# Selective scan in a four-layer kernel: read-out in half steps over seven groups, a fourth decay buffer, input loads in three pieces, and one group's decay products made twice

## The reference

```
delta = softplus(dt_proj(...))           # per token and channel d (256)
def step(h, inp):                        # h: 256 channels x 64 states
    dA = exp(dt[:, :, None] * A)
    h = dA * h + dt[:, :, None] * b[:, None, :] * xt[:, :, None]
    y = einsum('bdn,bn->bd', h, c)
```

## Time and profile before

| | us |
|---|---|
| median of 3 runs | 1350.41 (1347.94 to 1356.02) |
| the profiled execution: its own time | 1350.97 |
| its span, first to last instruction | 1349.1 |
| prepare stage, up to the first scan | 100.8 |
| scan stage, first scan to last | 622 |
| experts, attention, feed-forward | from about 758 to the end |

### The profile page before, as it was taken

One profiled execution on the slowest core, in us unless ns is written; L12 is line 12 of the kernel. 1 busy time (PEld: TensorE's weight loads), 2 busy tenths in 40 slices (PEclk: granted clock), 3 DMA queues, 4 the chain that ended last, 5 costly groups with the idle time before them and its releaser, 6 DMA issues.

```text
span 1349.1 us, 29055 instructions
## 1 busy us (share of the span) xinstructions
PE 1126.4 (83%) x11730; PEld 726.6 (54%) x11730; DVE 846.0 (63%) x1006; ACT 500.5 (37%) x1245; POOL 306.3 (23%) x930
## 2 busy tenths in 40 slices
PE   3647787889878887788886499999999597999998
PEld 2535444444444554454543288887777344465665
DVE  5859989899999999899995211112111477842211
ACT  3865554556555655555553011111111110121110
POOL 9641222222223222422232211111111200000000
PEclk8865868776888779876877599999999797999999
DMA  3897235433223222312214652222210400000000
GB/s 105 244 281 209 61 87 134 107 98 103 52 58 90 47 51 56 90 36 48 59 50 155 203 200 79 77 93 94 97 43 16 133 1 0 0 8 8 17 16 16
DMA packets 171685, 111.99 MB, mean 83 GB/s; under 512 B 93637, under 2 KB 162248, under 8 KB 169248
## 3 DMA queue, kind: packets, MB, share of 16 engines
q1 hardware_dynamic: 163120, 88.69, 23.7%
q0 software_dynamic: 8000, 20.87, 4.7%
q10 hardware_dynamic: 432, 0.59, 0.2%
HBM read 63.18 MB, written 45.90 MB: 81 GB/s over the span
## 4 chain that ended last, share of the span: by engine, by line
PE 52%; DVE 21%; issue 9%; SPq 7%; ACT 5%; DMA 3%; POOL 2%; DVEq 0%; POOLq 0%; ACTq 0%
DVE h L1151 13%; PE psum L1401 10%; PE psum L1413 10%; PE psum L1885 8%; PE psum L935 5%; PE psum L1896 4%; PE psum L921 4%; ACT decay L1036 3%; PE psum L902 3%; DVE den L1715 2%; PE psum L1841 2%; SPq L278 2%; DMA xdiag<-x_parts_d 1%; SPq L201 1%; SPq L199 1%
## 5 line engine op out<-in xcount | busy, mean ns | idle before, releaser
L1151 DVE TENSOR_TENSOR_SCAN h<-decay,psum 128x1024 f32<-128x1024 f32 x256 | 568.6, 2269 | 41.9 <-ACT psum L1046 34.5
L1036 ACT ACTIVATE decay<-psum 128x512 f32<-128x512 f32 x512 | 279.2, 600 | 211.1 <-PE psum L902 108.8
L921 PE MATMUL psum<-xdiag,bstat 96*128 96x64 bf16 x4096 | 199.9, 211 | 59.3 <-DVE h L1151 57.9
L921 PEld LDWEIGHTS psum<-xdiag,bstat 96*128 96x128 bf16 x4096 | 166.0, 109 | 86.7 <-DVE h L1151 77.3
L902 PEld LDWEIGHTS psum<-rows,shared 32*128 32x128 bf16 x4096 | 90.0, 104 | 221.2 <-issue 114.2
L935 PE MATMUL psum<-h,cstat 128*32 128x512 f32 x1024 | 187.2, 814 | 1.0 <-ACT y_raw L1088 1.0
L902 PE MATMUL psum<-rows,shared 32*128 32x64 bf16 x4096 | 123.9, 207 | 46.5 <-ACT decay L1036 38.0
L1401 PE MATMUL psum<-xdt,shared 128*128 128x320 f32 x512 | 141.4, 438 | 0.7 <-ACT xdt L1460 0.7
L1306 POOL TENSOR_TENSOR carry<-decay,h 128x16 f32<-128x16 f32 x240 | 57.9, 241 | 366.6 <-ACT decay L1036 366.4
L1413 PE MATMUL psum<-shared,hid 128*128 128x256 f32 x640 | 139.5, 379 | 0.6 <-ACT hid L1454 0.6
L1413 PEld LDWEIGHTS psum<-shared,hid 128*128 128x128 f32 x640 | 121.2, 190 | 17.0 <-issue 1.1
(11 more groups left out here) (192 smaller groups left out, 1044.1 us busy)
## 6 DMA issues: line engine op xcount, KB each, us to landing
shared<-in_w SPq DMA_DIRECT2D x16, 1024.0 KB, 4.8
xdiag<-x_parts_d SPq DMA_DIRECT2D x256, 48.0 KB
x_parts_d<-x_parts POOLq DMA_DIRECT2D x46, 256.0 KB, 8.0
parts_d<-dt_parts SPq DMA_DIRECT2D x24, 256.0 KB, 9.4
rows<-parts_d SPq DMA_DIRECT2D x128, 48.0 KB
disp_d<-zero SPq DMA_DIRECT2D x4, 1305.0 KB, 8.2
xd<-disp_d SPq DMA_DIRECT2D x8, 652.5 KB, 6.2
picked_d<-zero SPq DMA_DIRECT2D x4, 1024.0 KB, 5.7
```

The lines of the kernel that those rows point to most:

```text
L921: ins = pe.q.matmul(to.rearrange("p d (s e) -> p s d e", e=2), bstat[0:ROWS, c % 2, b, :], xdiag[0:ROWS, c % 2, b, :, d, :], start=True, s ...
L1036: act.q.activation(decay[:, gi % NB, 8 * half:8 * half + 8, :], per_d(bank_a[half]), ACT.Exp).then_inc(sem("exp"), 1)
L1151: dve.q.tensor_tensor_scan(out=h[:, half_slot(c, half), ch:ch + G, :].rearrange("p d t -> p (d t)"), data0=decay[:, gi % NB, :, :].rearran ...
```

## The change

Four things change in the scan stage; nothing else does.

1. `LOADS`: the same 14 loads in three pieces (groups 0, 1, 2) instead of six (groups 0 to 5).
2. `NB` = 4: four buffers of decays and of carries instead of three. ACT's exponential of group gi waits for scan gi - 4.
3. `Y_STEPS`: the read-out in eight half steps (one half of the channels each, four matmuls with 256 moving columns) in seven groups; group 3 has two of them, group 7 none. `Y_PICK` = 9 puts `y_sel` one group later. The last chunk's read-out has four pairs of half steps where it had four steps.
4. In the group of an odd chunk that has no read-out, `decays` runs its 16 matmuls twice, with the same operands into the same places.

```diff
-LOADS = ((("dt", 0), ("dt", 1), ("dt", 2)), (("dt", 3), ("b", 0), ("b", 1)), (("x", 0), ("x", 1)), (("x", 2), ("x", 3)),
-         (("x", 4), ("x", 5)), (("x", 6), ("x", 7)))
+LOADS = ((("dt", 0), ("dt", 1), ("dt", 2), ("dt", 3), ("b", 0), ("b", 1)), (("x", 0), ("x", 1), ("x", 2), ("x", 3)),
+         (("x", 4), ("x", 5), ("x", 6), ("x", 7)))
-NB = 3
+NB = 4
-Y_STEPS = ((0,), (), (1,), (), (2,), (), (3,))
-Y_OUT, Y_PICK = 7, 8
+Y_STEPS = ((0,), (1,), (2,), (3, 4), (5,), (6,), (7,))
+Y_OUT, Y_PICK = 7, 9
-    for js in (js for js in Y_STEPS if js):
+    for js in ((0, 1), (2, 3), (4, 5), (6, 7)):
         yield ("y", CHUNKS - 1, js)
...
-                for i in range(8):
+                for i in (*range(8), *range(8)) if gi % (CT * GROUPS) == GROUPS + 2 else range(8):
...
-                first, last = sorted((half_slot(c, 0), half_slot(c, 1)))
-                for j in js:
+                slots_of_h = sorted((half_slot(c, 0), half_slot(c, 1)))
+                for half, j in (divmod(n, 4) for n in js):
                     for q in range(4):
                         tok = 16 * q + 4 * j
-                        ins = pe.q.matmul(bank_y[32 * q:32 * q + 32, :].rearrange("p (s d e) -> p s d e", s=2, e=4),
-                                          s["cstat"][:, tok // 4, :], h[:, first:last + 1:last - first, :, tok:tok + 4],
+                        to = bank_y[32 * q:32 * q + 32, 256 * half:256 * half + 256].rearrange("p (d e) -> p d e", e=4)
+                        ins = pe.q.matmul(to, s["cstat"][:, tok // 4, :], h[:, slots_of_h[half], :, tok:tok + 4],
                                           start=j == 0, stop=j == 3)
-                if js[-1] == 3:
+                if js[-1] == 7:
                     ins.then_inc(sem("y"), 1)
```

## The result

The changed kernel takes 1362.7 us (median of 20 runs, 1355.3 to 1367.2) against 1355.7 for the kernel before (20 runs, 1347.9 to 1361.2): a ratio of 1.0058, 95% interval 1.0042 to 1.0075. It is 0.6% slower where 1.4% faster was forecast. That lies within the 1% that a measurement was said to tell from no change, inside the stated range, but on the other side. The profiled execution has a span of 1363.6 us against 1349.1.

What follows compares the result with a forecast made beforehand. It took DVE's scans to bind, with PE late at half clock. From the profiled 1350.97 us it took 18 for DVE idle time, 1 for loads and 0.5 for the tail: 1331.5, so 1331 against the median; range 1317 to 1364.

Steps and rivals of the forecast that it cites:

- If they stay as they are: Scan stage, 139.6 to 700 us: the 34 half-clock stretches keep their lengths, leaving 8.5 us of DVE idle time.
- the double step: Two half steps in one group: 0.98 us more where it meets a lag, 3.5 us added in all.
- PEclk under 0.7: Sign against the forecast: mean PE clock in the middle of the scan stage, expected still near 0.79.
- DVE's idle time: Sign for the forecast: idle before the scans (L1151) between 139.6 and 700 us near 12 us, instead of 30.1.
- What bounds the kernel, and where it loses: Scan stage: DVE's scans bind at 2.22 us each; only DVE's idle time, 36.4 us, can be won, lost at half clock.
- The prices at half clock: PE in the scan stage: half step 1.06 us, group 2.49, slack ahead of DVE 0.97, used up in 3 to 4 groups.
- The loads: x rows PE waits for, moved forward on SP's queue: mostly inside the 18 us gain, about 1 us by itself.
- The fourth buffer: Removes ACT's wait for scan gi - 3, 0.22 us before L902; alone under 0.3 us per chunk at half clock.
- Decays twice: 16 more matmuls in one group in sixteen, without read-out: costs nothing, or 7 us if uncovered.
- Gain given back: Rival: falls as frequent but longer, half-clock share 0.60, 23 us idle; 1339 to 1356, say 1345 us; chance 0.27.
- Half clock sticks: Rival: plain half steps keep PE at half clock; 1390 us at 80% share, most of it at 1364 to 1400; chance 0.15.
- The clock stays full: Rival: even PE work keeps 2.4 GHz, DVE's idle time goes but for 2 us; 1317 us; chance 0.10.

Runs made afterwards that it cites:

- eighth experiment: Kernel before with three load pieces, four buffers, later y_sel, and decay matmuls run twice in the groups without read-out: 1364.9 us, ratio 1.0111.
- fifth experiment: Changed kernel with its eight half steps one after each of the eight groups, no pair, decays made once: 1437.2 us, ratio 1.0636 to the kernel before.
- second experiment: Kernel before with only the eight half steps in seven groups; three buffers, six load pieces, decays once: 1363.4 us, ratio 1.0100.
- ninth: Kernel before with only a fourth buffer of decays and carries: 1353.1 us, ratio 0.9991.
- tenth: Kernel before with only the three load pieces, y_sel where it was: 1347.6 us, ratio 0.9937.
- eleventh: Changed kernel with each group's decays made once: 1360.6 us, ratio 1.0044 to the kernel before.

## Why the prediction was wrong

The forecast of 1331 us failed above all in one step, "**If they stay as they are**": the 34 half-clock stretches, most of 3.4 or 6.8 us, were carried over into a kernel whose PE work has another shape. They didn't stay. In the changed kernel only three of 23 are 3.4 us long, one is 6.8, and nine are 10.2. Put through the prediction's own working (0.14 us of lag for each us at half clock, less 0.97 for each stretch), the stretches of the changed kernel between 139.6 and 700 us give 22 us of idle time instead of 8.5. With the 3.5 for the double step that makes 26, where 39.4 were measured (44.7 less the stall told below). The rest is the second term that was too small, the double step.

Of the signs of being wrong that the prediction gave, PEclk under 0.7 didn't come (0.73). The one that told was DVE's idle time, 44.7 us where it said near 12.

Point by point:

- *What bounds the kernel, and where it loses.* Right. In the profiled executions every change of time against the kernel before is, within 5 us, the change of DVE's idle time before L1151: 33.7 us idle at 1339.2, 58.3 at 1365.1, 125.4 at 1439.1.
- *The prices at half clock.* Right: half step 1.08 and 0.64 us (1.06 and 0.62 worked out), group 2.51 (2.49), pair 1.86 start to start (1.98), slack used up after three groups (3 to 4). With the slack used up, the 1.77 us by which the pair and the transpose delay the inputs reach DVE almost whole, as 1.71.
- *The double step*, "0.98 more where it meets a lag; I add 3.5". Too small. A stretch mostly ends with a pair (19 of 21), so the pair meets the largest lag; and in odd chunks the transpose, 0.62 us at half clock, stands in the same group and wasn't counted. The seventh scan of odd chunks alone lost 17.9 us.
- *The loads.* Right in kind. Only 1 us stood in the sum for them by itself, the rest lay in the 18 without a figure; 8.5 were measured, 5 to 12 by the interval of the ratio. In the changed kernel all eight x issues stand ahead of the zeros, and L961 waits for DMA 2.5 us in all, where it waited 22.5 in weight loads and matmuls together. y_sel came later as said, and no transpose in the scan waited for it:

```profile
232.50 3.76 SPq L201 DMA_DIRECT2D xdiag<-x_parts_d  x8
236.31 3.30 SPq L865 DMA_DIRECT2D y_sb<-y_raw  x4
239.65 0.60 SPq L875 DMA_DIRECT2D disp_d<-zero  x1
```

- *The fourth buffer*, under 0.3 us a chunk: right, nothing. *Decays twice*, nothing: right at 16 of them; 128 of them cost 25 us in the eighth experiment, so the room they seemed to have isn't there in general.
- *The rivals.* Two of them named what happened. "Gain given back" had the mechanism (falls that each last longer, ended by the double step or the projection), a share of 0.60 where 0.54 was measured, and 25 stretches where there are 23; it put the idle time at 23 us in the middle, and 44.7 were measured (39.4 without one stall, below), as it took the slack's full 0.97 from each stretch and left the pair out. "Half clock sticks" names the clock of the fifth experiment, which has no pair: share 0.80. Its price of 1390 for that share can't be compared with the 1437 us measured, since most of the idle time there is ACT's wait for the read-out. Against this rival stood that two half steps together are as long as the step after which the clock rose; the changed kernel bears that out, as nearly all of its stretches end with the pair. The row that should have weighed more was the one already there: inputs and decays alone, PE busy, and half clock from 100.8 to 118. A plain run of half steps looks like that stretch more than like the pair of groups in the earlier trace rows.
- *The clock stays full*: wrong, the middle was at half clock for 54% of the time. The Trainium skill (TensorE: Matmul & The Clock Gate, Part 1) has it that the clock goes down when the engine has been idle for a while and comes back when it is kept busy. These traces don't agree: in the fifth experiment the clock stayed down for 41 us with PE busy 91% of the time.

## What to carry to other kernels

Where TensorE's clock moves between its two levels, a change of spacing can be a change of clock: before PE work is evened out, look for the rows in which the clock rises and ask whether the work that stood there will still stand there in one piece. The sum of busy time, the count of matmuls and the length of idle gaps said nothing here; the spacing of the same instructions was worth 18 us, and redundant matmuls in the groups without read-out some 8. When a step moves, look also at which engine waits for its end: in the fifth experiment ACT's copy came to wait for it, and most of that version's idle time stands behind it. When rows at half clock carry a forecast, price the case in which their share moves as the first case, not as an afterthought, and put loads that a later stage waits for ahead of bulk fills on the same queue.

## What the runs showed of the hardware

- TensorE stayed at 1.2 GHz for 41 us while it was busy 37 of them (fifth experiment), through a row of half steps of 1.08 us, 2.5 us or more apart. In the kernel before, 33 of 34 half-clock stretches ended 1.9 to 4.0 us after the start of a read-out step of fp32 matmuls in one piece (1.94 us at half clock), but 13 such steps passed without ending one.
- 32-row and 96-row bf16 matmuls of the same 64 columns differ in what they do to the clock: doubling the former in half of the groups went with a share of 0.48 at half clock, doubling the latter with 0.18, from 0.42 without either (one profiled execution each; the medians of the whole program's clock are 0.845, 0.906 and 0.857).
- In the changed kernel's profiled execution PE issued its matmuls about 0.7 us apart from 409 to 414 us, with no wait that the profile shows; DVE lost 6.3 us there ("remote" and L921 in the first rows). Those of the ninth, tenth and eleventh experiments show "remote" idle time of 5.4, 4.3 and 5.5 us, that of before none. What it is stays open; the second experiment lost its time without such a stall in its profile, so it isn't needed for the 7 us between the medians.
